# A two-layer vision kernel: first image's residual, tables and maxima at other places in the order

## What is computed

```python
# layer 0: group norm, softmax attention with 4 heads of 32, projection, residual
x = x + out_proj(softmax(q.T @ k / sqrt(128)) @ v) + out_bias
# layer 1: linear attention over tokens, 8 heads of 16
t = tokens(x)
t = t + Wr @ ((softmax_l(K) @ V.T).T @ softmax_k(Q)) + br      # K, Q, V of layernorm(t)
# then 8 experts, the best two for each token
n = layernorm(t); p, e = top_k(softmax(n' @ router + rb), 2)   # n' = layernorm(n)
t = t + sum(p / sum(p) * expert[e](n'))
```

## Time and profile before

| | us |
|---|---|
| median of 3 runs | 350.51 |
| lowest and highest | 349.59 and 351.45 |
| the profiled execution | 353.42 |
| its span, first to last instruction | 351.7 |
| PE busy in it | 315.8 |
| DVE, ACT, POOL busy | 200.0, 195.1, 114.5 |
| mean granted PE clock | 0.927 of full speed |

### The profile page before, as it was taken

The page is one execution under the profiler, slowest core; times in us unless marked ns, Lnnn a source line. Parts: engine busy times, 40 slices in busy tenths (PEclk is TensorE's granted clock), DMA queues, the critical chain, the costliest instruction groups (busy, mean ns, idle before and its releaser), DMA issues.

```text
span 351.7 us, 6258 instructions
## 1 busy us (share of the span) xinstructions
PE 315.8 (90%) x1885; PEld 196.1 (56%) x1885; DVE 200.0 (57%) x620; ACT 195.1 (55%) x305; POOL 114.5 (33%) x192
## 2 busy tenths in 40 slices
PE   7979898899999999999999979894567699999985
PEld 3533533344444335355353244674567699999985
DVE  2586446475766844547547752767844157776610
ACT  2470576476767764455559520658144377878722
POOL 2074094000000000100030778004477855555630
PEclk9995999899999999999999975998659699999999
DMA  7069795927000008000000111300011422224215
GB/s 200 5 127 203 165 208 203 261 61 271 2 2 3 1 2 234 8 0 3 0 2 0 35 43 38 68 10 7 24 47 53 121 62 79 68 73 129 83 51 220
DMA packets 20540, 27.88 MB, mean 79 GB/s; under 512 B 3831, under 2 KB 14508, under 8 KB 20252
## 3 DMA queue, kind: packets, MB, share of 16 engines
q1 hardware_dynamic: 15800, 17.57, 18.7%
q0 software_dynamic: 3520, 9.39, 8.5%
q10 hardware_dynamic: 1188, 0.53, 0.6%
HBM read 11.15 MB, written 8.33 MB: 55 GB/s over the span
## 4 chain that ended last, share of the span: by engine, by line
PE 71%; DVE 12%; POOL 5%; issue 4%; ACT 3%; DMA 3%; DVEq 1%; SPq 0%; POOLq 0%; ACTq 0%
PE ps L919 17%; PE ps L896 9%; PE ps L1160 8%; PE ps L1138 7%; PE ps L877 5%; POOL expert_in L530 4%; PE ps L861 4%; PE ps L756 2%; PE ps L955 2%; PE ps L796 2%; PE ps L828 2%; DMA Qs<-mrow 1%; DVE pm L1275 1%; PE ps L946 1%; PE ps L1117 1%
## 5 line engine op out<-in xcount | busy, mean ns | idle before, releaser
L598 ACT ACTIVATE probs<-ps 128x1024 f32<-128x1024 f32 x64 | 65.3, 1021 | 34.1 <-PE ps L896 34.0
L919 PE MATMUL ps<-probs,vT 128*32 128x512 f32 x256 | 68.6, 612 | 0.6 <-ACT probs L598 0.5
L919 PE MATMUL ps<-probs,ones 128*32 128x512 f32 x256 | 68.6, 612 | 0.0
L466 POOL TENSOR_TENSOR rstd<-ve,minus_half 128x8 f32<-128x8 f32 (+1 forms) x8 | 11.0, 1385 | 144.1 <-DVE ve L1326 77.4
L1272 DVE CUSTOM_DVE_ANT_0 above<-ps,above 128x512 f32<-128x512 f32 x56 | 38.6, 691 | 29.9 <-PE ps L877 27.5
L1138 PE MATMUL ps<-w,GT 128*128 x312 | 45.0, 291 | 8.4 <-ACT GT L734 8.4
L536 POOL DMA_INDIRECT token_out<-Y,yidx x39 | 37.7, 967 | 31.1 <-DVE Y L1606 27.4
L1138 PEld LDWEIGHTS ps<-w,GT 128*128 128x128 f32 x312 | 40.9, 204 | 9.8 <-issue 9.7
L1160 PE MATMUL ps<-XTT,w1s 128*128 128x128 f32 x312 | 45.7, 294 | 0.2 <-ACT XTT L712 0.2
L896 PE MATMUL ps<-Qs,Ks 98*128 98x512 f32 x128 | 43.6, 422 | 2.3 <-DMA Qs<-mrow 1.6
L591 ACT ACTIVATE above<-ps 128x512 f32<-128x512 f32 x56 | 33.5, 599 | 19.4 <-PE ps L861 19.4
(11 more groups left out here) (233 smaller groups left out, 441.4 us busy)
## 6 DMA issues: line engine op xcount, KB each, us to landing
XR<-expert_in SPq DMA_DIRECT2D x39, 65.0 KB
Qs<-q_hi SPq DMA_DIRECT2D x16, 128.0 KB, 3.0
w<-in_L_ffn_W SPq DMA_DIRECT2D x1, 2048.0 KB, 8.5
w<-in_L_ffn_W SPq DMA_DIRECT2D x8, 256.0 KB, 4.4
YG<-token_out SPq DMA_DIRECT2D x8, 256.0 KB, 3.7
Ks<-k_hi SPq DMA_DIRECT2D x14, 128.0 KB, 2.8
expert_in<-zeros POOLq DMA_DIRECT2D x1, 1300.0 KB, 5.6
expert_in<-zeros POOLq DMA_DIRECT2D x1, 1235.0 KB, 8.2
```

The source lines that it names most:

```text
L598: nc.scalar.activation(probs[:, s % 3, :], bank(2 + 2 * (s % 2), 2), ACT.Exp).then_inc(exp_done, 1)
L919: last = nc.tensor.matmul(bank(value_bank(o))[i * HD:(i + 1) * HD, :], w, probs[:, s % 3, hd * HALF:(hd + 1) * HALF], start=kt == 0, stop= ...
```

## The change

Four things move; no arithmetic is added or removed.

1. "residual" goes from step 33 to 35, into one step with "project", and all later parts of image 0 go one step later. "centre" stays at 33.
2. The tables become a part of their own, v_tables. Image 0's run in the second chain, after image 1's norm_stats and ahead of F; image 1's stay behind its slots.
3. The second chain's power stands before column J - 4 of scatter(0), one pair of stores sooner.
4. The copies of the maxima k = 1 are issued by ScalarE in step 6, not by SP, so that SP has no wait between the stacks of unit 2 and those of unit 3.

```diff
+        SECOND_ROWS_AT = 6
...
-        LAYER1_AT = {BEGIN_LAYER1: "centre residual", 34: "project", 35: "tokens_stats tokens", 38: "keys",
-                     40: "keys_exp", 41: "query_value0", 42: "query_value1", 43: "keyT query_max",
...
-                     53: "gates_exp", 54: "route choose norm2_0", 55: "norm2_1", 56: "norm2_2 counts", 57: "norm2_3"}
+        LAYER1_AT = {BEGIN_LAYER1: "centre", 35: "residual project", 36: "tokens_stats tokens", 39: "keys",
+                     41: "keys_exp", 42: "query_value0", 43: "query_value1", 44: "keyT query_max",
...
+                     54: "gates_exp", 55: "route choose norm2_0", 56: "norm2_1", 57: "norm2_2 counts", 58: "norm2_3"}
...
-        LAYER1_DVE = {"before": "tokens_stats tokens query_value0 query_value1 keys queries queries_scaled context fold",
-                      0: "attend stats", 1: "logits shift route choose", 2: "counts"}
+        LAYER1_DVE = {"before": "tokens_stats first_tables tokens query_value0 query_value1 keys queries queries_scaled context fold",
+                      0: "attend stats", 1: "logits shift route choose", 2: "counts tables"}
...
             stacks(2)
-            max_rows(0, 1)
             stacks(3)
...
-            scatter(0, lambda j: rsqrt(B + 2) if j == J - 3 else None)
+            scatter(0, lambda j: rsqrt(B + 2) if j == J - 4 else None)
...
+            def first_unit_rows(qh):
+                act.wait_ge(mrow_ready, qh + 1)
+                for hd in range(2):
+                    dst = Qs[SPLIT:STACK, 0, head(0, hd), qh * HALF:(qh + 1) * HALF]
+                    act.dma_start(dst.bitcast(f32).rearrange("s (t q) -> s t q", t=QH),
+                                  mrow[hd * 2 * QH:(hd + 1) * 2 * QH, :].bitcast(f32)).then_inc(mrow_in[qh], 16)
+
+            first_unit_rows(0)
...
+                if s == SECOND_ROWS_AT:
+                    first_unit_rows(1)
                 run_parts(layer1, LAYER1_AT, s, 0)
...
+            def v_tables(b):
+                full, full_end, first_of, rest, mixed, jump, take, tail, space = (cnt[:, i, :] for i in range(9))
                 t0, t1 = TABLES[b]
...
-                      "counts": [v_slots]}
+                      "counts": [v_slots], "tables": [v_tables], "first_tables": [lambda b: v_tables(0)]}
```

More of the change, by code:

```diff
@@ L307, in build_program @@
         CLOSE_LAST = UNITS * STEPS - 4
-        LAYER1_AT = {BEGIN_LAYER1: "centre residual", 34: "project", 35: "tokens_stats tokens", 38: "keys",
-                     40: "keys_exp", 41: "query_value0", 42: "query_value1", 43: "keyT query_max",
-                     44: "keyT_sb queries_exp", 45: "queries context", 46: "queries_scaled fold", 47: "queryT",
-                     48: "queryT_sb", 49: "attend stats", 50: "tokenT", 51: "tokenT_sb", 52: "logits shift",
-                     53: "gates_exp", 54: "route choose norm2_0", 55: "norm2_1", 56: "norm2_2 counts", 57: "norm2_3"}
+        LAYER1_AT = {BEGIN_LAYER1: "centre", 35: "residual project", 36: "tokens_stats tokens", 39: "keys",
+                     41: "keys_exp", 42: "query_value0", 43: "query_value1", 44: "keyT query_max",
+                     45: "keyT_sb queries_exp", 46: "queries context", 47: "queries_scaled fold", 48: "queryT",
+                     49: "queryT_sb", 50: "attend stats", 51: "tokenT", 52: "tokenT_sb", 53: "logits shift",
+                     54: "gates_exp", 55: "route choose norm2_0", 56: "norm2_1", 57: "norm2_2 counts", 58: "norm2_3"}
         LAYER1_PE = {"before": "residual project query_value0 query_value1 keys values keyT", "first": "queryT context",
                      0: "fold attend", "1 mid": "tokenT", 1: "logits", 2: "counts"}
-        LAYER1_DVE = {"before": "tokens_stats tokens query_value0 query_value1 keys queries queries_scaled context fold",
-                      0: "attend stats", 1: "logits shift route choose", 2: "counts"}
+        LAYER1_DVE = {"before": "tokens_stats first_tables tokens query_value0 query_value1 keys queries queries_scaled context fold",
+                      0: "attend stats", 1: "logits shift route choose", 2: "counts tables"}
         LAYER1_ACT = {"before": "tokens_stats", "staged": "queries_exp keys_exp values keyT_sb", "0 mid": "queryT_sb",
```

## The result

| | kernel before | kernel after |
|---|---|---|
| median, us | 350.85 | 358.73 |
| lowest and highest | 349.59 and 354.05 | 357.22 and 359.04 |
| the profiled execution, its span | 353.42, 351.7 | 357.73, 356.0 |

The ratio is 1.0205 (95% interval 1.0168 to 1.0242): 7.9 us slower by the medians, where 350.7 was forecast and 352.8 was the end of the range. In the code after the change, the lines quoted from 896 on stand 5 further down (L896 is L901), from 1501 on 7.

What follows compares the result with a forecast made beforehand. TensorE was taken to bound the kernel, through its idle time. Terms -0.8, 0, +0.1 and +1.0 made +0.3, less about 0.1 for the clock: +0.2 on the median 350.51, 350.7 us; own range 349.5 to 352.0, eight-in-ten 348.2 to 352.8.

Steps and rivals of the forecast that it cites:

- Part 1, -0.8: Step 33: moving the residual removes TensorE's 0.78 us wait for rw; -0.8 us, between -0.8 and 0.
- These are not awaited yet: Image 0's slots: GpSimd's stores start at 195.2 instead of 194.36 us, and nothing waits for them yet.
- Part 2, 0: Second chain: the 3.28 us tables delay F, but F still ends before TensorE wants it; 0 us.
- the 2.7 us of cover: Second chain: the margin between F ending at 214.3 us and TensorE wanting it at 217.0 us.
- Part 3, +0.1: Second chain's power two stores sooner: last store and XR's loads come 2.1 us later; +0.1 us, between 0 and 0.5.
- Even: First XR tile there at 225.1 us, second 0.46 later, TensorE transposing at 225.4 us: practically no wait.
- With eight it waits as now: GpSimd's power: with eight stores ahead, ending at 206.7 us, it still waits for the variance, ready at 208.8 us.
- Part 4, +1.0: Step 8: earlier stacks delay the zero fill's end and the second maxima behind it; +1.0 us, between -1.8 and +3.
- stacks in front: Slower rival, 0.18: unit 3's remaining stacks precede the fill's end, maxima land 2.5 to 3 us later; 352.6 to 354.3 us.
- The maxima go after it: Step 8: the second maxima's copies move only after the second zero fill, which ends at about 65 us.
- Copies on time: Faster rival, 0.21: ScalarE's queue is served between fill pieces, maxima arrive before TensorE asks; 346.9 us, or 348.7 without the clock.
- the 0.8 is not there: Late XR or another wait at step 35 eats the step 33 gain; 351.5 us, inside the forecast's own range, no separate chance.

Runs made afterwards that it cites:

- p1_only: The kernel before with only the residual moved to step 35 and all later layer parts one step later; measured 351.30 us, ratio 1.0005.
- before_b: The kernel before, unchanged, profiled once more; the profiled execution took 349.42 us, span 347.7 us, mean granted clock 0.941.

## Why the prediction was wrong, point by point

The path behind the first chain failed: the forecast had TensorE reach XR no sooner than XR was there. Here TensorE waited 4.64 us for it, and with the clock up 1.2 to 1.3 us in the kernel before. At step 8 the cause was right and the size too small.

- **Part 1, -0.8: right to the chain's end, wrong behind it.** The wait of step 33 is gone and the chain ends 0.9 sooner. "These are not awaited yet", of the stores that come one step later, is the step that failed. They are awaited through XR, which in p1_only comes 1.2 later against the chain. Beside part 3 that step is taken up by the power's wait for the variance.
- **Part 2, 0: nothing in the runs speaks against it.** F's first user waits 0.28 us, for F itself; the 2.7 us of cover are gone, for the same reason as below.
- **Part 3, +0.1: the largest error.** XR's delay was sized fairly: two stores of 1.43 us, 2.9 against the chain, where part 3 alone measured 2.8 and the whole change 3.8, with the long last store that the sum didn't have. "Even" failed. TensorE's arrival at 225.4 was read from an execution whose bias matmuls had taken 7.19 us at half clock. With 3.88 us, in before_b, it arrives at 220.5, and any further lateness of XR is added to a wait. A row of busy TensorE was taken for work, where PEclk beside it read 0.51; the sum was then added to a median of executions that, by their clock, mostly don't have that stretch. "With eight it waits as now" held: GpSimd waited 1.74 us for the variance, where the forecast's own times (206.7 and 208.8) give 2.1.
- **Part 4, +1.0: right cause, too small.** The wait grew by 1.70 us, inside the ends of -1.8 and +3; on top came a clock of 0.57 from 66 to 74, where the trace that was read has it to 70 only the earlier trace rows and before_b has 1.00. The term had no price for that; only "stacks in front" had one, 1.7. The amount of stacks beside the fill, one stack and as much again, was too little: the fill ended 5 us later, not 1. "The maxima go after it" failed too, and this kept the wait from growing by as much: they went through while the fill still ran. "They are issued 1.1 us later" is wrong: 60.10 against 59.80 for the cast, ahead of the maximum part at 60.57.
- **The rivals.** "Stacks in front" (352.6 to 354.3, from a start behind 68.0) comes nearest for part 4 alone, 352.77, although in the changed kernel step 8 starts at 67.59. "Copies on time" is refuted: no packet of the copies ran before 64.4. Its mechanism, service between pieces of the fill, was there, but late. Nor was the fill one packet for each engine, as the forecast's side of that rule has it: the earlier trace rows counts 114 in 2.8 us. Why SP's copies got none of that time stays open. By the Trainium skill, DMA: Bandwidth & Descriptors, section "Issuing engines are not separate DMA queues", a second issuer gains the issue time only; the trace agrees in that nothing landed sooner, with ScalarE's issue 0.30 us behind the cast as SP's had been. No rival had XR as the end with a price: "the 0.8 is not there" names it and gives it 351.5.
- **The two errors add up**, and a third comes with them: behind a wait of 4.6 us the clock was at 0.51 from 227 to 234, which is most of the 2.3 us behind XR (5.21 us for queryT and context, 2.99 in before_b). Part 1 or part 3 alone has most of this already: 4.67 and 4.66 us behind waits of 2.06 and 2.42. The text's own sign of a wrong forecast, a new wait of TensorE between 134 and 226, came at 223.8.

## What to carry to other kernels

Before a wait is called absent, look at the clock of the stretch in front of it: an engine that is busy at half clock hides who would be waited for at full clock, and one profiled execution above the median is a hint to take another. Where an engine's fixed series of stores ends in a load that all wait for, moving a waiting instruction forward in that series adds its wait to the end. And a transfer that is kept off a bulk fill by an accidental wait of its issuer should not be set free without moving the fill.

## What the runs showed of the hardware

- Half clock under a fully busy TensorE: 14.00 us of 14.00 busy from 206 to 220 at 0.51, through eight matmuls of one contraction row (7.19 us) and the filler. In before_b the stretch reads 0.88, and the eight take 3.88 us.
- ScalarE's DMA issue stood ahead of its arithmetic: the first copy's issue began at 60.10 while exponentials ran from 59.65 to 60.67, and ahead of the relu of 60.57, which stands before it in ScalarE's program.
- The stacks and the fill share the engines' time: q0 had 96.8% in the earlier trace rows, and 69 to 74% with unit 3's stacks beside it.
- GpSimd's store beside VectorE's product QV took 1.64 to 1.86 us in four traces, and ended 0.83 to 0.84 us behind the product; the stores before it took 0.96 to 1.10.
